# Second network weight's butterflies on GpSimd in the second attention, third raw weight buffer for the experts

## The chip, the cores and the metric

The kernel runs on one core of a Trainium2 chip. The engines are TensorE (PE), VectorE (DVE), ScalarE (ACT), GpSimd (POOL) and SyncE (SP), with 16 DMA engines. DMAs are issued by SP, by ACT (small ones) and by POOL (the indirect ones). The metric is the device time of one execution in microseconds; lower is better.

## The reference, cut to what matters

A decoder of two layers on `x` of shape (4, 512, 512) in float32. Each layer has three steps, each on the layernorm of what came before and added to it:

```python
x = x + _L0_attn_ref(_layernorm(x), ...)             # attention with a linear memory, 16 heads
x = x + _L0_xattn_ref(ctx_512, _layernorm(x), ...)   # learned graph over the tokens
x = x + _L0_ffn_ref(_layernorm(x), ...)              # experts: 32 routed, top 8 of 64, 512 -> 2*256 -> 512
x = x + _L1_attn_ref(_layernorm(x), ...)             # attention
x = x + _L1_xattn_ref(_layernorm(x), ctx_512, ...)   # causal attention over the context
x = x + _L1_ffn_ref(_layernorm(x), ...)              # network 512 -> 2048 -> 512 with a Hadamard transform
```

The last one is `hidden = silu(x @ W1.T) * (x @ W3.T)`, then `out = fwht(hidden) @ W2.T`. `fwht` is the Walsh-Hadamard transform over the 2048 hidden columns: in 11 rounds it takes pairs `a`, `b` to `a + b` and `a - b`. It is linear, so the kernel applies it to the weight W2 in place of `hidden`. An expert computes `silu(g) * u` from `x @ w_gate_up`, and multiplies by `w_down`.

## The kernel before, in words

Six stages follow each other, each with its own block of code per engine: `attention_linear` (0 to about 680 us), `graph_and_router` (to about 1103 us), `experts` (to about 1488 us), `attention_layers` (two attentions, self and causal, to about 2425 us) and `network`. Engines are ordered by semaphores alone; each engine runs its instructions in the order written. SP issues one DMA after the other, and whatever it waits for holds up everything behind it; POOL likewise, where compute and indirect DMAs are one queue.

**The second network weight.** W2 (512 by 2048) is transformed in two parts. In the graph stage "asides" do the first 7 rounds: TensorE multiplies transposed chunks of 128 hidden columns by a 128x128 Hadamard matrix, ACT scales the result into one of three buffers `aside_out` (128 x 512), and SP stores it to `w2T` in HBM (`aside_store`, 16 stores of 256 KB). The last 4 rounds (`STAGES`) mix the 16 chunks. Before, this was done in `experts`: SP loads a tile of 128 output columns of all 16 chunks (`load_w2`, 1 MB in 512-byte pieces, 4 tiles) into `shared_rows`, DVE does 4 stages of two instructions each (`butterfly`, one instruction after each of the 32 experts, 128 x 1024 elements) between the two halves of `shared_x`, and SP stores the result to `w2_mixed` (`store_w2`, 1 MB), which the network reads.

**The experts.** For each of 32 experts e, in the order of TensorE: transposes of the gathered rows of e+2 (L2367), gate and up products of e+1 (48 matmuls in three passes of high and low parts, L50 to L52), down products of e (12). Weights come raw from HBM by SP (`first_gu`, 1 MB, and `first_d`, 512 KB, two buffers each, by the parity of e), ACT casts the high part (L2419, L2423), DVE subtracts for the low part of gate-up (L2455), POOL for the low part of down (L2518). Gate-up's and down's loads of an expert both wait (L2327, L2328, in Signal's L176) until DVE and POOL have split the expert two before. POOL's order for expert e is

```python
gather(e + 4)                      # two indirect DMAs, rows of x into ex_rows
split_d(e // 2 + 1, e % 2)         # the low part of down's weights, expert e + 2
scatter(e)                         # waits for y of e and for the landing of scatter e - 1
```

where the scatter adds 256 rows of y to `x_rows` in HBM. ACT and DVE write the gated y (L2441, L2486) into SBUF, two buffers.

**The attentions.** 32 steps g (8 batches, of which 4 are causal, times 4 groups of 4 heads), with lead-in steps from -3. In step g TensorE does the scores of g (L440) for the exponentials of ACT, the scores of g+1 (L420) for the maxima of DVE (L657), the weighed values and sums of g (L454, L463), at the end of the step the maxima's transpose (L431) and the projections of g+3. Three pairs of PSUM banks go round. ACT copies the weighed values and sums of g-1 at the start of step g (L604, L607); before the copy of values it waits until POOL has made `oT` of g-2 in the step before. DVE takes reciprocals of the sums (L682) and POOL multiplies them into `oT` (L766), once a step. The output projection of a batch (L532) follows in the first step of the next batch (steps 5, 9, ...), after POOL's `oT` of its last group. POOL also makes `rstd` once a batch, and masks in the causal half. SP's `stack` issues 12 DMAs of 128 KB (L336) for the scores of g+3 at the end of each step.

## Time and profile before

| | us |
|---|---|
| median of 3 timed runs | 2962.68 (2962.14 to 2963.93) |
| the profiled execution | 2967.87 |
| its span, first to last instruction | 2966.1 |

| engine | busy us | share of the span |
|---|---|---|
| TensorE matmul | 2490.3 | 84% |
| DVE | 1781.1 | 60% |
| ACT | 1225.8 | 41% |
| POOL | 791.4 | 27% |

Mean granted clock of TensorE 0.908 of full speed. The busy shares are means over stages with different limits, so they have to be read stage by stage. The durations of single instructions in the text are those of the profiled execution, which took 5.2 us more than the median.

### The profile page before, as it was taken

The numbers are of one execution on the slowest core, as the hardware profiler recorded it, in microseconds if no ns is written. First come the engines' busy times: TensorE is split into PE (matmuls) and PEld (weight loads), VectorE is DVE, ScalarE is ACT, GpSimd is POOL, SyncE is SP. The second block draws the span as 40 slices with busy tenths as digits, with TensorE's granted clock in tenths as the row PEclk, the third lists the DMA queues.
The fourth block names the chain that finished last, engine by engine and source line by source line (L and its number), as shares of the span: only waits on it lengthen the run. The fifth ranks groups of instructions, "written<-read, shape, count | busy, mean of one in ns | idle before, by whom it ended". The sixth has DMA issues, their size and how long they took to land. (4 is left out here: it accounts for less than half of the span.)

```text
span 2966.1 us, 34593 instructions
## 1 busy us (share of the span) xinstructions
PE 2490.3 (84%) x12822; PEld 1652.2 (56%) x12822; DVE 1781.1 (60%) x2772; ACT 1225.8 (41%) x1859; POOL 791.4 (27%) x1054
## 2 busy tenths in 40 slices
PE   5899999984344369889769999999999879999999
PEld 4554545421222248788645454545555548888887
DVE  3766666546799977777636655655565444444443
ACT  3343434335766725455314333443433223333332
POOL 2223232213566626878600000001211110000000
PEclk8999999986666679999879999999999889999999
DMA  3313132202222357999732323333533331101000
GB/s 108 77 44 86 44 86 47 68 19 94 85 94 90 111 186 221 268 255 268 188 95 65 93 72 78 91 97 94 128 88 94 115 125 67 43 1 43 1 29 15
DMA packets 177017, 287.09 MB, mean 97 GB/s; under 512 B 20769, under 2 KB 52385, under 8 KB 176866
## 3 DMA queue, kind: packets, MB, share of 16 engines
q1 hardware_dynamic: 159458, 249.73, 28.7%
q0 software_dynamic: 14336, 34.61, 5.4%
q8 instruction: 88, 1.44, 0.2%
q10 hardware_dynamic: 3072, 0.79, 0.1%
q14 instruction: 63, 0.52, 0.1%
HBM read 149.79 MB, written 58.98 MB: 70 GB/s over the span
## 5 line engine op out<-in xcount | busy, mean ns | idle before, releaser
L657 DVE TENSOR_REDUCE at_negmax<-at_ps 128x2 f32<-128x1024 f32 (+3 forms) x256 | 259.2, 1017 | 131.5 <-PE at_ps L420 66.6
L572 ACT ACTIVATE at_probs<-at_ps 128x1024 f32<-128x1024 f32 (+3 forms) x256 | 221.8, 866 | 265.3 <-PE at_ps L440 262.5
L1258 DVE TENSOR_REDUCE a_negmax<-a_ps 128x2 f32<-128x1024 f32 x128 | 155.2, 1217 | 137.4 <-PE a_ps L1011 136.8
L50 PE MATMUL ff_ps<-ff_xnT_hi,ff_s_hi 128*128 128x512 f32 x512 | 201.0, 393 | 5.1 <-DVE ff_xnT_lo L2782 5.1
L52 PE MATMUL ff_ps<-ff_xnT_hi,ff_s_lo 128*128 128x512 f32 x512 | 200.2, 391 | 0.0
L51 PE MATMUL ff_ps<-ff_xnT_lo,ff_s_hi 128*128 128x512 f32 x512 | 200.1, 391 | 0.0
L1842 ACT ACTIVATE gr_act_signs<-gr_signed,gr_test 128x512 bf16<-128x512 f32 x248 | 177.3, 717 | 25.6 <-POOL gr_test L2221 14.0
L1159 ACT ACTIVATE a_probs<-a_ps 128x1024 f32<-128x1024 f32 x128 | 130.9, 1024 | 137.8 <-PE a_ps L1029 137.3
L2812 DVE TENSOR_TENSOR ff_hid<-ff_hid,ff_ps 128x512 f32<-128x512 f32 x64 | 44.0, 688 | 238.8 <-ACT ff_hid L2757 238.8
L440 PE MATMUL at_ps<-at_qk 98*128 98x512 f32 (+3 forms) x512 | 171.7, 417 | 17.6 <-DMA at_qk<-at_mrow 10.8
L440 PEld LDWEIGHTS at_ps<-at_qk 98*128 98x128 f32 x512 | 83.1, 193 | 158.7 <-issue 89.9
L420 PE MATMUL at_ps<-at_qk 96*128 96x512 f32 (+3 forms) x512 | 161.0, 378 | 11.7 <-DVE at_xnT_lo L718 8.0
L2757 ACT ACTIVATE ff_hid<-ff_ps 128x512 f32<-128x512 f32 x64 | 38.3, 598 | 303.6 <-PE ff_ps L52 303.6
L50 PE MATMUL ex_ps<-ex_x_hi,ex_gu_hi 128*128 128x256 f32 x512 | 151.5, 296 | 4.9 <-issue 4.9
L2536 POOL DMA_INDIRECT x_rows<-ex_y,ex_index_out x64 | 134.7, 2104 | 56.0 <-DMA x_rows<-ex_y,ex_index_out 38.8
L51 PE MATMUL ex_ps<-ex_x_lo,ex_gu_hi 128*128 128x256 f32 x512 | 148.3, 290 | 0.0
L52 PE MATMUL ex_ps<-ex_x_hi,ex_gu_lo 128*128 128x256 f32 x512 | 147.9, 289 | 0.0
L766 POOL TENSOR_TENSOR at_oT<-at_weighed 128x512 f32<-128x512 f32 x32 | 40.8, 1274 | 382.4 <-DVE at_weighed L682 382.4
L750 POOL TENSOR_SCALAR_AFFINE_SELECT at_probs<-at_probs 128x256 f32<-128x256 f32 x128 | 52.6, 412 | 291.6 <-ACT at_probs L572 291.6
L682 DVE RECIPROCAL at_weighed<-at_weighed 128x128 f32<-128x128 f32 x128 | 119.9, 940 | 15.3 <-ACT at_weighed L607 15.3
L727 DVE TENSOR_TENSOR at_part<-at_ps,at_part 128x512 fp32r<-128x512 f32 x64 | 43.4, 692 | 142.3 <-ACT at_part L628 142.3
L532 PE MATMUL at_ps<-at_wo,at_oT 128*128 128x512 f32 x256 | 115.9, 607 | 6.8 <-POOL at_oT L766 6.6
(416 smaller groups left out, 6425.9 us busy)
## 6 DMA issues: line engine op xcount, KB each, us to landing
at_qk<-at_part SPq DMA_DIRECT2D x384, 128.0 KB, 2.3
first_gu<-in_L_ffn_w_gate_up_dram SPq DMA_DIRECT2D x32, 1024.0 KB, 6.2
a_qk<-a_part SPq DMA_DIRECT2D x192, 128.0 KB, 2.3
first_d<-in_L_ffn_w_down_dram SPq DMA_DIRECT2D x32, 512.0 KB, 7.8
gr_aside_raw<-in_L_ffn_W_dram SPq DMA_DIRECT2D x48, 256.0 KB, 3.3
w13T<-gr_aside_out SPq DMA_DIRECT2D x32, 256.0 KB, 3.2
shared_x<-x_after_cross SPq DMA_DIRECT2D x8, 1024.0 KB, 8.0
ff_slab<-w13T SPq DMA_DIRECT2D x14, 512.0 KB, 6.3
```

Of the source, the lines that this page charges most:

```text
L50: pe.matmul(out, lh, rh, start=start, stop=False, skip_group_check=True)
L51: pe.matmul(out, lh, rl, start=False, stop=False, skip_group_check=True)
L52: return pe.matmul(out, ll, rh, start=False, stop=stop, skip_group_check=True)
L420: mm = pe.matmul(bank(key, i, 0, n), qk[0:KROWS, g % STACKS, 0, j, t * P:(t + 1) * P], qk[0:KROWS, g % STACKS, 1, j, 0:n], start=True, sto ...
L440: mm = pe.matmul(bank(key, i, lo), qk[0:KROWS + 2, g % STACKS, 1, j, t * P:(t + 1) * P], qk[0:KROWS + 2, g % STACKS, 0, j, lo:S], start=Tr ...
L572: act.activation(probs[:, t % 2, 2 * w:2 * w + 2, lo:S], banks(("kq", g, s), lo), ACT.Exp, scale=SCALE).then_inc(free(("kq", g, s)), 1)
L657: dve.reduce_max(negmax[:, g % 2, :].rearrange("p (j t) -> p j t", t=NT)[:, 2 * w:2 * w + 2, t], banks(("qk", g, s), 0, width(g, t)), AX.X ...
L682: dve.reciprocal(weighed[:, 1, t * P:(t + 1) * P], weighed[:, 1, t * P:(t + 1) * P]).then_inc(rec_done, 1)
L1159: act.activation(probs[:, t % 2, 2 * w:2 * w + 2, :], banks(("kq", g, s)), ACT.Exp, scale=SCALE).then_inc(free(("kq", g, s)), 1)
L1258: dve.reduce_max(negmax[:, g % 2, :].rearrange("p (j t) -> p j t", t=NT)[:, 2 * w:2 * w + 2, t], banks(("qk", g, s)), AX.X, negate=True).t ...
L1842: act.activation(act_signs[:, j, :], src, ACT.Sign, scale=-1.0, bias=against, accum_out=total[:, i, j:j + 1]).then_inc(counted_to[j], 1)
L2536: pool.indirect_dma_start(x_rows, bass.IndirectOffsetOnAxis(index_out[:, at:at + 1], 0), y[:, u, t, :], None, compute_op=ALU.add).then_inc ...
```

## The change

Three things. First, the last 4 stages of the second weight leave the experts and go to POOL in the self attention, as 8 tiles of 64 output columns (`W2_COLS`), at steps -1, 0, 2, 3, 4, 6, 7 and 8. At each it runs 8 instructions of 128 x 512 elements, before `oT` of that step. SP loads the next tile (512 KB, now whole rows of 4 KB, as `w2T` has a new layout) and stores the finished one (512 KB in 256-byte pieces) at the head of a step. The second stage of a tile waits for the previous tile's store, since its buffer is overwritten. Second, the asides' stores to `w2T` go in 256-byte pieces, to fit the new layout. Third, the experts' raw weights get a third buffer in `shared_x`, and the buffers are taken by e modulo 3; the gate-up load waits for DVE's split of expert e-3 alone, the down load for POOL's. The network's loads of its first chunks also wait for the last store.

```diff
+        W2_STEPS = (-1, 0, 2, 3, 4, 6, 7, 8)
+        w2_raw, mix = got[:, 0].rearrange("p k d -> p (k d)"), [got[:, 1 + i].rearrange("p k d -> p (k d)") for i in range(2)]
...
+            def load_w2(n):
+                if n:
+                    sp.wait_ge(mixed, 2 * STAGES * (n - 1) + 2)
+                sp.dma_start(w2_raw, w2T.rearrange("(t p) e -> t p e", p=P)[n]).then_inc(w2_in, 16)
+
+            def store_w2(n):
+                sp.wait_ge(mixed, 2 * STAGES * (n + 1))
+                sp.dma_start(w2_mixed.rearrange("(k p) (t c) -> t p k c", p=P, c=W2_COLS)[n],
+                             mix[(STAGES - 1) % 2].rearrange("p (k c) -> p k c", c=W2_COLS)).then_inc(w2_out, 16)
...
+                sp.wait_ge(w2_out, 16 * len(W2_STEPS))
...
             load(sp, 0)
             load(sp, 1)
+            load_w2(0)
             for g in STEPS:
                 b, c = g // NC, g % NC
+                if g - 1 in W2_STEPS:
+                    store_w2(W2_STEPS.index(g - 1))
+                if g in W2_STEPS[:-1]:
+                    load_w2(W2_STEPS.index(g) + 1)
...
+            def butterflies(n):
+                for stage in range(STAGES):
+                    src, dst = mix[(stage - 1) % 2] if stage else w2_raw, mix[stage % 2]
+                    a, b, c, d = (m.rearrange("p (g h k) -> p g h k", h=2, k=W2_COLS << stage)[:, :, h, :] for m in (src, dst) for h in range(2))
+                    if stage == 0:
+                        pool.wait_ge(w2_in, 16 * (n + 1))
+                    if stage == 1 and n:
+                        pool.wait_ge(w2_out, 16 * n)
+                    if n or stage:
+                        pool.wait_ge(mixed, 2 * (STAGES * n + stage))
+                    pool.tensor_tensor(c, a, b, ALU.add).then_inc(mixed, 1)
+                    pool.tensor_tensor(d, a, b, ALU.subtract).then_inc(mixed, 1)
+
             rstds(0)
             for g in STEPS:
+                if g in W2_STEPS:
+                    butterflies(W2_STEPS.index(g))
...
-            w13_parts, w2_parts = w13T.rearrange("(k p) (m e) -> k m p e", p=P, m=2), w2T.rearrange("(k p) d -> k p d", p=P)
+            w13_parts, w2_parts = w13T.rearrange("(k p) (m e) -> k m p e", p=P, m=2), w2T.rearrange("(t p) (k c) -> k p t c", p=P, c=W2_COLS)
...
+        raw_gu, raw_d = [first_gu[:, 0], first_gu[:, 1], shared_x[:, 0]], [first_d[:, 0], first_d[:, 1], shared_x[:, 1, 0:I_DIM // P, :]]
+        RAWS = len(raw_gu)
...
-            load(1, 0)
-            load_w2(0)
-            for i in range(PAIRS - 2):
-                load(i + 1, 1)
-                load(i + 2, 0)
-                if i % STAGES == 2:
-                    load_w2(i // STAGES + 1)
-                if i % STAGES == 0 and i:
-                    store_w2(i // STAGES - 1)
-            load(PAIRS - 1, 1)
-            store_w2(NT - 1)
-            sp.wait_ge(w2_out, 16 * NT)
+            def load(e):
+                r, i, u = e % RAWS, (e - RAWS) // 2, (e - RAWS) % 2
+                if e >= RAWS:
+                    gu_lo_done[u].wait(sp, i, 1)
+                sp.dma_start(raw_gu[r], gu_dram[e]).then_inc(w_in[r], 16)
+                if e >= RAWS:
+                    d_lo_done[u].wait(sp, i, 1)
+                sp.dma_start(raw_d[r], d_dram[e]).then_inc(w_in[r], 16)
...
             for e in range(E_ROUTED):
                 body(e // 2, e % 2, e + 2 < E_ROUTED)
-                butterfly(e)
```

## Rows read from the trace of the kernel before

**Rows 1.** Windows: from:to, length, busy (x instructions) by engine, clock, DMA share, GB/s.
```profile
1106.00:1150.00 44.00, 33.36 (x213) 31.59 (x214) 23.12 (x20) 19.93 (x20) 24.07 (x15) 0.77 0.61 193
1150.00:1440.00 290.00, 263.55 (x1815) 242.82 (x1814) 224.92 (x186) 149.71 (x160) 233.38 (x133) 0.95 0.96 263
1440.00:1489.00 49.00, 26.93 (x153) 22.49 (x151) 25.05 (x20) 10.81 (x14) 23.86 (x13) 0.81 0.58 112
...
1640.00:1760.00 120.00, 116.87 (x574) 61.16 (x573) 67.16 (x84) 44.79 (x52) 6.12 (x5) 1.00 0.30 77
```

**Rows 2.** Groups of lines, 1150 to 1440: busy us, mean ns | idle before, ended by.
```profile
L2536 POOL DMA_INDIRECT x_rows<-ex_y,ex_index_out x52 | 111.2, 2139 | 39.8 <-DMA x_rows<-ex_y,ex_index_out 29.7 <-issue 10.1
...
L2518 POOL TENSOR_TENSOR ex_d_lo<-first_d,ex_d_hi 128x1024 fp32r<-128x1024 f32 x27 | 65.2, 2415 | 0.6
L2545 POOL DMA_INDIRECT ex_rows<-normed,index x54 | 58.1, 1075 | 16.5 <-issue 16.5
L2419 ACT CAST ex_gu_hi<-first_gu 128x2048 fp32r<-128x2048 f32 x27 | 51.6, 1910 | 35.0 <-DMA first_d<-in_L_ffn_w_down_dram 35.0
...
L2367 PE MATMUL ex_ps<-ident,ex_rows 128*128 128x128 f32 x208 | 31.1, 298 | 23.1 <-DMA ex_rows<-normed,index 22.9 <-issue 0.2
...
L2498 DVE TENSOR_TENSOR shared_x<-shared_x 128x1024 f32<-128x1024 f32 x20 | 24.3, 1215 | 8.2 <-DMA w_mixed<-shared_x 8.2
...
L2498 DVE TENSOR_TENSOR shared_x<-shared_rows 128x1024 f32<-128x1024 f32 x7 | 8.5, 1211 | 0.0
```

**Rows 3.** Waits of SP, 1110 to 1480: us in total, times, longest.
```profile
SPq L176 <- POOL ex_d_lo L2518: 295.6, 30, 22.7
```

**Rows 4.** Timeline, one load: start, us, engine, line [idle before <-releaser].
```profile
1261.39 2.42 POOL L2518 TENSOR_TENSOR ex_d_lo<-first_d,ex_d_hi 128x1024 fp32r<-128x1024 f32 x1
...
1263.89 0.37 SPq L2329 DMA_DIRECT2D first_gu<-in_L_ffn_w_gate_up_dram  x1
...
1274.26 1.91 ACT L2419 CAST ex_gu_hi<-first_gu 128x2048 fp32r<-128x2048 f32 x1 [2.52 <-DMA first_d<-in_L_ffn_w_down_dram]
```

**Rows 5.** DMA, 1150 to 1440: packets; queues; issues with KB and landing us.
```profile
DMA packets 45266, 76.30 MB, mean 263 GB/s; under 512 B 2651, under 2 KB 14939, under 8 KB 45259
...
q1 hardware_dynamic: 33255, 47.31, 50.8%
q0 software_dynamic: 12004, 28.93, 45.1%
...
shared_rows<-w2T SPq DMA_DIRECT2D x3, 1024.0 KB, 15.0
...
x_rows<-ex_y,ex_index_out POOLq DMA_INDIRECT x52, 7.8
```

**Rows 6.** End of the experts: timeline of DVE, and waits of 1440 to 1490.
```profile
1444.49 4.37 DVE L2498 TENSOR_TENSOR shared_x<-shared_x 128x1024 f32<-128x1024 f32 x1
...
1455.75 4.38 DVE L2498 TENSOR_TENSOR shared_x<-shared_x 128x1024 f32<-128x1024 f32 x1
...
PE ex_ps L50 <- DVE ex_h_lo L2455: 5.9, 3, 3.9
```

**Rows 7.** Attention: POOL by line; timelines of POOL, SP, ACT; landings.
```profile
L766 POOL TENSOR_TENSOR at_oT<-at_weighed 128x512 f32<-128x512 f32 x32 | 40.8, 1274 | 382.4 <-DVE at_weighed L682 382.4
...
1677.14 1.28 POOL L766 TENSOR_TENSOR at_oT<-at_weighed 128x512 f32<-128x512 f32 x1 [23.06 <-DVE at_weighed L682]
...
1663.52 7.63 SPq L336 DMA_DIRECT2D at_qk<-at_part  x12
...
1687.87 0.59 ACT L604 COPY at_weighed<-at_ps 128x512 f32<-128x512 f32 x1 [0.46 <-PE at_ps L454]
...
w2T<-gr_aside_out SPq DMA_DIRECT2D x16, 256.0 KB, 2.0
...
x_after_attn<-at_res SPq DMA_DIRECT2D x8, 512.0 KB, 2.9
```

More of the change, by code:

```diff
@@ L21 @@
 HID = 2048
+W2_COLS = 64
 HC = P // HD
@@ L241, in attention_layers @@
         staged, ctx_sb = got[:, 0], got[:, 1, 0, :].rearrange("p (t l) -> p t l", l=L)
+        STAGES = (HID // P).bit_length() - 1
+        W2_STEPS = (-1, 0, 2, 3, 4, 6, 7, 8)
+        assert len(W2_STEPS) == D // W2_COLS and W2_STEPS[-1] < NC * (B - 2) + 1
+        w2_raw, mix = got[:, 0].rearrange("p k d -> p (k d)"), [got[:, 1 + i].rearrange("p k d -> p (k d)") for i in range(2)]
+        w2_in, w2_out, mixed = sem("w2_in"), sem("w2_out"), sem("mixed")
         above, above_r = got[:, 1, 1, 0:P], wkT[0][:, 1, 0:P]
@@ L2274, with experts @@
 I_DIM = 256
-def experts(nc, env, tag, normed, index, x_rows, w_gate_up, w_down, w2T, w2_mixed, raw_gu, raw_d, shared_x, shared_rows):
+def experts(nc, env, tag, normed, index, x_rows, w_gate_up, w_down, first_gu, first_d, shared_x, shared_rows):
     F = 2 * I_DIM // P
@@ L2322, in _ @@
         def _(sp):
-            def load(i, u, weights=True):
-                e = i * 2 + u
-                if not weights:
-                    return
-                gu_lo_done[u].wait(sp, i, 0)
-                d_lo_done[u].wait(sp, i, 0)
-                sp.dma_start(raw_gu[:, u], gu_dram[bass.ds(e, 1)].rearrange("e p c f -> (e p) c f")).then_inc(w_in[u].sem, 16)
-                sp.dma_start(raw_d[:, u], d_dram[bass.ds(e, 1)].rearrange("e p c f -> (e p) c f")).then_inc(w_in[u].sem, 16)
-            def load_w2(n):
-                if n:
-                    sp.wait_ge(mixed, 2 * STAGES * (n - 1) + 2)
-                sp.dma_start(w2_raw[:].rearrange("p (k c) -> p k c", c=P), w2_tiles[n]).then_inc(w2_in, 16)
-            def store_w2(n):
-                sp.wait_ge(mixed, 2 * STAGES * (n + 1))
-                sp.dma_start(mixed_tiles[n], mix[:, (STAGES - 1) % 2, :].rearrange("p (k c) -> p k c", c=P)).then_inc(w2_out, 16)
-            for u in range(2):
-                load(0, u, weights=False)
-                sp.sem_inc(w_in[u].sem, 32)
-            load(1, 0)
-            load_w2(0)
-            for i in range(PAIRS - 2):
-                load(i + 1, 1)
-                load(i + 2, 0)
-                if i % STAGES == 2:
-                    load_w2(i // STAGES + 1)
-                if i % STAGES == 0 and i:
-                    store_w2(i // STAGES - 1)
-            load(PAIRS - 1, 1)
-            store_w2(NT - 1)
-            sp.wait_ge(w2_out, 16 * NT)
+            def load(e):
[6 more added lines that the diff above has]
+                sp.dma_start(raw_d[r], d_dram[e]).then_inc(w_in[r], 16)
+            for r in range(2):
+                sp.sem_inc(w_in[r], 32)
+            for e in range(2, E_ROUTED):
+                load(e)
         @block.tensor
@@ L2416, in split_gu @@
             def split_gu(i, u):
-                w_in[u].wait(act, i, 32)
+                e = 2 * i + u
+                act.wait_ge(w_in[e % RAWS], 32 * (e // RAWS + 1))
                 gu_ready[u].wait(act, i, 0)
-                act.copy(flat(gu_hi[:, u]), flat(raw_gu[:, u])).then_inc(gu_hi_done[u].sem, 1)
+                act.copy(flat(gu_hi[:, u]), flat(raw_gu[(2 * i + u) % RAWS])).then_inc(gu_hi_done[u].sem, 1)
             def split_down(i, u):
                 y_ready[u].wait(act, i, 0)
-                act.copy(flat(d_hi[:, u]), flat(raw_d[:, u])).then_inc(d_hi_done[u].sem, 1)
+                act.copy(flat(d_hi[:, u]), flat(raw_d[(2 * i + u) % RAWS])).then_inc(d_hi_done[u].sem, 1)
             def split_x(i, u):
@@ L2458, in split_gu @@
                 gu_hi_done[u].wait(dve, i, 1)
-                low(flat(gu_lo[:, u]), flat(raw_gu[:, u]), flat(gu_hi[:, u]), gu_lo_done[u])
+                low(flat(gu_lo[:, u]), flat(raw_gu[(2 * i + u) % RAWS]), flat(gu_hi[:, u]), gu_lo_done[u])
             def keep_gate(i, u):
@@ L2486, in body @@
                 dve.tensor_scalar(y[:, u, 1, :], ps[:, 7, :], gate[:, (2 * i + u) % 4, 1:2], None, ALU.mult).then_inc(y_dve[u].sem, 1)
-            def butterfly(n):
-                row, stage, half = n // (2 * STAGES), n // 2 % STAGES, n % 2
-                src, dst = mix[:, (stage - 1) % 2, :] if stage else w2_raw[:], mix[:, stage % 2, :]
-                a, b, c, d = (m.rearrange("p (g h k) -> p g h k", h=2, k=P << stage)[:, :, h, :] for m in (src, dst) for h in range(2))
-                if stage == 0 and half == 0:
-                    dve.wait_ge(w2_in, 16 * (row + 1))
-                if stage == 1 and half == 0 and row:
-                    dve.wait_ge(w2_out, 16 * row)
-                if n:
-                    dve.wait_ge(mixed, n)
-                dve.tensor_tensor((c, d)[half], a, b, (ALU.add, ALU.subtract)[half]).then_inc(mixed, 1)
             dve.tensor_scalar(empty[:], index[:], 0.5, None, ALU.is_lt).then_inc(emptied, 1)
@@ L2517, in split_d @@
                 d_hi_done[u].wait(pool, i, 1)
-                pool.tensor_tensor(flat(d_lo[:, u]), flat(raw_d[:, u]), flat(d_hi[:, u]).bitcast(F32), ALU.subtract
+                pool.tensor_tensor(flat(d_lo[:, u]), flat(raw_d[(2 * i + u) % RAWS]), flat(d_hi[:, u]).bitcast(F32), ALU.subtract
                                    ).then_inc(d_lo_done[u].sem, 1)
```

22 lines of the change are left out of this document (11 added, 11 removed).

## The prediction

> **What bounds the kernel now.** I read the busy table by stage first, because the change touches three stages and leaves the rest alone. In the experts' steady part, 1150 to 1440 us, four things stand close together [rows 1]: TensorE is busy 263.6 of 290 us at a granted clock of 0.95 (of the 2.4 GHz level), the DMA engines 0.96 of the time at 263 GB/s, POOL 233.4 us, DVE 224.9 us. In the attention that follows (1640 to 1760) it is TensorE alone, 116.9 of 120 us at clock 1.00, with POOL at 6.1 us.
>
> Next I read the groups of lines of that steady part, for what ended each idle time [rows 2]. TensorE's waits of any size there are 22.9 us of the transposes L2367, for gathered rows that have not landed. Those gathers are issued by POOL, and POOL is nearly full: its 233.4 us of work and 27 us of issue gaps (10.1 + 16.5 + 0.6, the idle in front of L2536, L2545 and L2518; L2536's is 39.8 less 29.7 of DMA) make 260.6, and the other 29.7 us it waits for the previous expert's scatter to land. ACT meanwhile waits 35.0 us at L2419 for raw weights. About 26.6 experts pass here (L2419 27 times, L2536 52 times two to an expert), so an expert takes 10.9 us.
>
> Why the weights are late stands in the waits of SP [rows 3] and in one stretch of time [rows 4]. SP waits 295.6 us, 30 times, always for POOL's `d_lo` split, since both loads of an expert wait for it. POOL does that split at 1261.39 to 1263.81, SP issues the load at 1263.89, and ACT's cast of the next expert but one, which uses that buffer, stands at 1274.26 after 2.52 us of waiting. So in practice a load has one period to land, not two.
>
> The DMA section of the same stretch says how full the engines are and with what [rows 5]: queue q1 takes 50.8% of 16 engines, q0 (gathers and scatters) 45.1%. The second weight's tiles go in pieces of 512 bytes: 3 loads and 3 stores of 1 MB, that is 12,288 packets and 6.29 MB of q1's 33,255 and 47.31. One such load lands after 15.0 us.
>
> **The change, part by part, and what it costs.**
>
> *Experts, steady part.* Removed: 27 DVE butterflies at 1.21 us, 32.8 us, and the 8.2 us that they waited for the store [rows 2]; six of the eight 1 MB transfers. DVE is not the bound, so the 41 us are no gain as such. What counts is the DMA demand. By bytes the w2 pieces are 6.29/47.31 of 50.8%, or 6.8% of the engines' 290 us, 19.6 us. By packets it would be 12,288/33,255, 54 us; a 512-byte piece surely takes less time than a 2 KB one, so I take the bytes. If the DMA engines stay at 0.96, 19.6 us less demand shortens the part by 20.4 us. Moved: the three-deep ring lets expert e's load start after the split of e-3, and its gate-up half no longer waits for POOL's split. That gives a load one period (10.9 us) more; the longest wait in [rows 4] was 2.5 us, so I expect the 35.0 us of ACT to go entirely. What is late next is POOL: 260.6 us of work and gaps, then TensorE at 263.6. So 26.4 us is the ceiling and 0 the floor, if scatter's landing keeps its pace. I take 17: the 20.4, less a sixth, since three resources within 3% of each other do not all run full. Term: -17.
>
> *Experts, both ends.* At the start SP loads w2 (1 MB) in front of expert 3's weights; at 263 GB/s that is 4 us of engine time. Part of it is hidden, I take -2 (bounds 0 and -4). At the end two butterflies last 4.4 us in place of 1.2 [rows 6], because POOL's split of two SBUF tensors runs at the same time; `hid` of the next expert stands behind them, and TensorE waits 5.9 us in three places for `h_lo`. With the butterflies gone I take -4 (bounds 0 and -8: the 5.9 and some 2 us of the last 1 MB store, which runs beside the last scatters). Term: -6.
>
> The Trainium skill (SBUF — State Buffer, Who interferes with whom) says that a DVE instruction with two SBUF inputs and a GpSimd instruction that reads SBUF shut each other out. The 4.4 against 1.2 us of [rows 6] agrees. By it the move takes two-input work off DVE where POOL is full, and in attention the DVE lines that could meet the butterflies are few, since maxima, splits and residuals read PSUM; it leaves the sum as it is.
>
> *Attention, POOL.* Added: 8 tiles of 8 instructions over 128x512. POOL's product of two SBUF tensors of that shape, L766, takes 1.27 us [rows 7], so 64 x 1.274 = 82 us, 10.2 a tile, on an engine that is idle 113.9 of 120 us. Queued behind them on POOL: `oT` of the step before and `rstd`. Who waits: ACT's copy L604 and the output projection. The narrow places are tiles 4 and 7 (steps 4 and 8). In step 4 the store of tile 3 is issued by SP only after the twelve `stack` DMAs, at 1671.2; butterflies after the first stage wait for it. If it lands 5 us after, six more instructions end at 1683.8, and `oT`, now at 1677.1, ends at 1685.1. ACT's copy stands at 1687.9 [rows 7]. That is 2.8 us of slack. Landing of a store of this size from attention is 2.9 us with 2 KB pieces, and 15.0 is the worst that any w2 transfer shows [rows 5, 7]. At 15 us `oT` would end at 1695.1: 7.2 us late, twice; with 1.3 us each for tiles 3 and 6, an estimate (their step leaves more room), 17 us together. I take 5 us to land and no loss there, and 1 us for SP's 16 more issues and 8 MB more traffic. Term: +1 (bounds 0 and +17).
>
> The Trainium skill (DMA: Bandwidth & Descriptors, Specifications) wants pieces of 512 bytes or more, with read-modify-write below; here w2 goes to HBM in 256-byte pieces in two places. This speaks against the change; no row of this trace has a 256-byte store. Were such a store twice as slow as the 2.9 us one, 5.8 us, it would still end inside the slack.
>
> *Attention, the rest.* The reciprocals and the layernorm of DVE read SBUF alone, one tensor each, and may meet butterflies. `rstd` stands behind tiles 1, 4 and 7 on POOL and is used only in the next step. SP's new wait in front of the network's chunks is for stores that end at step 9 of 34. I take 0, and keep as the far end that each butterfly delays DVE by its whole length, 82 us.
>
> *Graph stage.* Sixteen stores of 256 KB of the second weight now go in 256-byte pieces. They land in 2.0 us now [rows 7]; three output buffers cover them, and even 4 us is shorter than the spacing of three asides. I take 0, bounds 0 and 16 x 1 us.
>
> **Sum.** -17 - 6 + 1 + 0 = -22 us. The profiled execution took 2967.9 us (span 2966.1), so 2945.9; it lies 5.2 us above the median of the three timed runs, 2962.7, which gives 2940.7.
>
> **Rivals.**
>
> *The scatter chain holds the pace.* Each scatter waits for the previous one's landing; one issue of 2.1 us, then the second's landing of 7.8 us make 9.9 us [rows 2, 5], near the period of 10.9 already. Then ACT's wait for weights goes and POOL's stays. For it: the 29.7 us [rows 2]. Against: landing depends on the same full DMA engines. It leaves 5 of the 17: -10, 2952.7. Chance 0.17.
>
> *TensorE's floor is reached.* All 26.4 us of idle go, ends -8, attention 0: -34, 2928. For it: no resource but POOL is then above TensorE. Against: POOL's 260.6. Chance 0.13.
>
> *oT is late in attention.* The 256-byte store lands in 15 us: +17 in place of +1, so -6, 2956.7, no change that can be measured. It decides from 7.8 us of landing on. Against: the DMA engines are little used there. Chance 0.07.
>
> *DVE is held by POOL in attention.* This one ends slower. If POOL's butterflies shut DVE out for their whole length, 82 us of DVE are added over eight steps. TensorE waits for DVE's maxima bank by bank, with 3 banks to cover; with half of it exposed, +41 on -22 is +19, 2982. It decides once more than 22 us are exposed. For it: [rows 6]. Against: there both instructions read two SBUF tensors, and DVE's large lines in attention read PSUM. Chance 0.06.
>
> **How the numbers follow.** My forecast has 0.57; its own range is -10 to -32, 2931 to 2953. Range for 8 in 10: from 2928 (the TensorE floor) to 2957, which takes in the scatter chain and late `oT`. A measurement of this kernel tells 0.2%, 5.9 us, from no change. Faster than 2956.8: the forecast, the floor, and nearly all of the scatter case, 0.85; within 0.2%: most of late `oT` and the rest of the scatter case, 0.08; slower 0.07.
>
> **What the profile after would show.** Right: the experts' stage shorter by some 23 us; no wait of L2419 for first_d; DMA share still above 0.93 with fewer bytes; TensorE's share there above 0.95; in attention 64 POOL instructions near 1.27 us and TensorE's steps unchanged. Wrong: L2536 still waiting 30 us for its own landing, L604 or L532 waiting for `oT`, or DVE's maxima L657 and reciprocals L682 longer than before. The prediction fails most easily at the 17, which rests on how three nearly full resources share what is freed.

## The result, and the profile after

The changed kernel takes 2970.41 us (median), the kernel before 2960.11 us in the runs beside it: ratio 1.0031, 95% interval 1.0021 to 1.0040. It is slower by 0.3%, where 0.7% faster was forecast, and outside the forecast range. The profiled execution has a span of 2977.0 us against 2966.1.

One number first on how far single profiles carry. In eighteen later profiles the code ahead of the experts is the same, and yet the experts' first instruction stands anywhere from 1094.8 to 1109.6 us. So I compare lengths of stages, and let medians of many runs decide on the whole. A stage's length varies too: a second profile of the same changed kernel (`after_again`) has 381.2 us for the experts where the first has 389.6, so a difference of a few us between two single profiles is no result by itself.

The borders of the stages are single instructions: the experts' iota, the next block's first load, the first `stack` (here of the kernel after; before they stand at 1103.51, 1488.65 and 1515.73):

```profile
1104.08 0.14 POOL L2553 IOTA ex_spare_rows<- 128x2 int32 x1 [43.27 <-POOLq L45]
```

```profile
1493.65 0.92 SPq L225 DMA_DIRECT2D shared_x<-x_rows  x2
...
1523.56 6.42 SPq L342 DMA_DIRECT2D at_qk<-at_part  x10
```

The experts' stage takes 1493.65 - 1104.08 = 389.6 us (before 385.1; 381.2 in `after_again`), where some 23 less were forecast. From there to the first `stack` of the attention it is 29.9 us (before 27.1). The rest, up to the feed-forward's cast of `xnT_hi`, is 914.3 us (before 911.2; kernels with the same code there lie between 909.9 and 914.3, so these 3.1 us are no result).

The busy table of the steady part, to be read beside [rows 1]: length, busy us (x instructions) of PE, PEld, DVE, ACT and POOL, granted clock, DMA share, GB/s.

```profile
1150.00:1440.00 290.00, 256.66 (x1780) 234.49 (x1778) 211.42 (x157) 144.09 (x157) 205.28 (x130) 0.97 0.93 238
```

The groups of lines of the same stretch, which answer to [rows 2]:

```profile
L2542 POOL DMA_INDIRECT x_rows<-ex_y,ex_index_out x52 | 90.0, 1730 | 68.5 <-DMA x_rows<-ex_y,ex_index_out 60.6 <-issue 7.9
...
L2474 DVE TENSOR_TENSOR ex_gu_lo<-first_gu,ex_gu_hi 128x2048 fp32r<-128x2048 f32 x18 | 79.7, 4430 | 9.7 <-ACT ex_gu_hi L2438 9.7
...
L2385 PE MATMUL ex_ps<-ident,ex_rows 128*128 128x128 f32 x208 | 30.1, 291 | 33.3 <-DMA ex_rows<-normed,index 33.3
```

And its transfers, which answer to [rows 5]:

```profile
DMA packets 32365, 68.92 MB, mean 238 GB/s; under 512 B 2483, under 2 KB 2483, under 8 KB 32358
...
q1 hardware_dynamic: 20717, 40.75, 48.1%
q0 software_dynamic: 11641, 28.11, 45.1%
...
first_gu<-in_L_ffn_w_gate_up_dram SPq DMA_DIRECT2D x18, 1024.0 KB, 7.8
first_d<-in_L_ffn_w_down_dram SPq DMA_DIRECT2D x18, 512.0 KB, 4.4
...
x_rows<-ex_y,ex_index_out POOLq DMA_INDIRECT x52, 8.2
ex_rows<-normed,index POOLq DMA_INDIRECT x52, 6.2
```

What the reader is to see: the work did go away (DVE 13.5 us less, 7.4 MB less, no line waits for weights), and yet no more experts pass: 52 scatters, as before. From the end of one expert's second scatter issue to the next's it is 11.17 us on average (before 11.04, a little more than the prediction's 10.9; 10.93 in `after_again`), worked out from POOL's timelines. I call this the spacing. DMA share fell only from 0.96 to 0.93 while the rate fell from 263 to 238 GB/s. POOL now waits 60.6 us for its own scatters (29.7 before), TensorE 33.3 us for gathered rows (22.9), and `gu_lo` takes 4.43 us where it took 2.81 (the line of the kernel before):

```profile
L2455 DVE TENSOR_TENSOR ex_gu_lo<-first_gu,ex_gu_hi 128x2048 fp32r<-128x2048 f32 x26 | 73.1, 2810 | 30.5 <-ACT ex_gu_hi L2419 30.5
```

A gate-up load lands in 7.8 us (6.2 before), a scatter in 8.2 (7.8), gathered rows in 6.2 (5.5).

At the attention's start, the timeline of the kernel after:

```profile
1503.62 1.25 POOL L785 TENSOR_TENSOR shared_rows<-shared_rows 128x512 f32<-128x512 f32 x1
1503.67 5.70 DVE L671 TENSOR_SCALAR shared_x<-shared_x,at_mv,at_rstd 128x512 f32<-128x512 f32 x4 [1.17 <-POOL at_rstd L766]
1504.84 1.44 POOL L786 TENSOR_TENSOR shared_rows<-shared_rows 128x512 f32<-128x512 f32 x1
```

The four layernorm instructions of DVE take 5.70 us together, in the kernel before 1.92:

```profile
1498.55 1.92 DVE L649 TENSOR_SCALAR shared_x<-shared_x,at_mv,at_rstd 128x512 f32<-128x512 f32 x4 [1.17 <-POOL at_rstd L744]
```

GpSimd's first butterfly starts 0.05 us ahead of them.

### The profile page after: what moved, and what is told of

The parts are those of the page before. It is cut to its first block and busy times, and to the rows that moved or that the text cites. A ratio compares the mean times of both kernels' runs of the same rounds, so it can differ in the third digit from the quotient of the medians.

```text
span 2977.0 us, 34609 instructions
## 1 busy us (share of the span) xinstructions
PE 2487.8 (84%) x12822; PEld 1647.6 (55%) x12822; DVE 1765.1 (59%) x2740; ACT 1223.5 (41%) x1859; POOL 846.0 (28%) x1118
## 5 line engine op out<-in xcount | busy, mean ns | idle before, releaser
L1884 ACT ACTIVATE gr_act_signs<-gr_signed,gr_test 128x512 bf16<-128x512 f32 x248 | 177.3, 717 | 25.4 <-POOL gr_test L2263 10.6
L2542 POOL DMA_INDIRECT x_rows<-ex_y,ex_index_out x64 | 112.9, 1764 | 82.9 <-DMA x_rows<-ex_y,ex_index_out 72.8
L476 PE MATMUL at_ps<-at_probs,at_v 128*32 128x512 f32 (+3 forms) x1024 | 118.9, 537 | 0.7 <-POOL at_probs L772 0.5
```

The costliest lines, as they stand in the source:

```text
L476: mm = pe.matmul(ps[j * HD:(j + 1) * HD, NUM, lo:S], v[:, g // NC % 2, t, c * P + j * HD:c * P + (j + 1) * HD], probs[:, t % 2, j, lo:S], ...
L1884: act.activation(act_signs[:, j, :], src, ACT.Sign, scale=-1.0, bias=against, accum_out=total[:, i, j:j + 1]).then_inc(counted_to[j], 1)
```

## Experiments

"Stage" is from the experts' iota to the next block's first load, in one profile; "landing" the median of scatters and of gathers in 1150 to 1440; "GU" how long after the end of the last gather's issue SyncE issues the gate-up load, in most periods (worked out from the timelines of POOL and SP); the ratio is to the kernel before, with its 95% interval.

| version | ratio | stage us | landing us | GU us |
|---|---|---|---|---|
| before | 1 | 385.1 | 7.8, 5.5 | 2.5 |
| after | 1.0031 (1.0021-1.0040) | 389.6 | 8.2, 6.2 | 4.6 |
| after_again | 1.0020 (1.0007-1.0033) | 381.2 | 8.0, 6.0 | 4.6 |
| two_raw | 0.9975 (0.9962-0.9987) | 373.4 | 7.1, 5.1 | 2.5 |
| paired | 0.9983 (0.9971-0.9995) | 375.2 | 7.5, 5.5 | 2.5 |
| start_wait | 1.0024 (1.0011-1.0037) | 382.7 | 8.1, 6.2 | 4.6 |
| norm_first | 1.0007 (0.9994-1.0020) | 381.3 | 8.1, 6.2 | 4.6 |
| split_two | 1.0008 (0.9998-1.0017) | 381.3 | 8.2, 6.1 | 4.6 |
| late_down | 0.9985 (0.9974-0.9995) | 376.7 | 7.5, 5.4 | 2.5; nine at 2.8-5.1 |
| d_first | 0.9997 (0.9987-1.0007) | 374.3 | 7.7, 5.5 | 2.9 |
| gu_delayed | 1.0003 (0.9993-1.0013) | 376.0 | 7.9, 5.6 | 3.0 |
| both_late | 0.9990 (0.9979-1.0000) | 375.2 | 7.6, 5.5 | 2.5 |
| gu_landing | 0.9992 (0.9978-1.0006) | 374.6 | 7.7, 5.6 | 2.9 |
| both_landing | 0.9979 (0.9967-0.9991) | 373.6 | 7.9, 5.7 | 2.5-4.5 |
| apart | 1.0026 (1.0012-1.0041) | 388.6 | 8.5, 6.3 | 4.9 |
| pair_then_split | 1.0015 (1.0000-1.0029) | 380.6 | | |
| split_then_pair | 1.0010 (0.9995-1.0025) | 377.3 | | |
| no_weights | 2947.1 us, one run | 363.2 | 5.2, 4.8 | |
| two_norm | 0.9970 (0.9960-0.9980) | 371.4 | 7.2, 4.9 | 2.5 |
| three_norm | 0.9970 (0.9958-0.9982) | 373.5 | 7.5, 5.4 | 2.5 |

The versions fall into two groups. "Split" are those in which the gate-up load waits for `gu_lo` alone throughout: after, after_again, start_wait, norm_first, split_two, apart. "Paired" are the ten, other than no_weights, in which both loads wait for both low parts. In 1150 to 1440 the spacing is 10.93 to 11.17 us in the six split profiles and 10.59 to 10.69 in the ten paired ones, and POOL waits 46.9 to 62.5 us for its scatters to land in the split ones, 12.3 to 25.2 in the paired ones (29.7 before). These two measures part the groups more clearly than the length of the stage.

### The change taken apart: two_raw and paired

The pairing, in both:

```diff
                 if e >= RAWS:
                     gu_lo_done[u].wait(sp, i, 1)
+                    d_lo_done[u].wait(sp, i, 1)
                 sp.dma_start(raw_gu[r], gu_dram[e]).then_inc(w_in[r], 16)
-                if e >= RAWS:
-                    d_lo_done[u].wait(sp, i, 1)
                 sp.dma_start(raw_d[r], d_dram[e]).then_inc(w_in[r], 16)
```

and in two_raw `raw_gu, raw_d = [first_gu[:, 0], first_gu[:, 1]], [first_d[:, 0], first_d[:, 1]]`.

> The changed kernel with two raw weight buffers and the old pairing (both low parts read, then both loads issued); what is left of the change is that the second network weight's transfers and butterflies are in the attention. Theory crowding (mine now): the third buffer buys nothing, because the pace of the steady part is that of the row traffic and the scatters, and its earlier loads lengthen gathers and scatters. Then the first transposes come back from 1114.2 to about 1110, the experts' stage falls from 389.6 us to 376 to 384, and the kernel is 5 to 13 us faster than the changed one (about 2957 to 2965). Rival, buffer is worth it: the weights wait of ScalarE (35 us before) comes back, the stage grows to 393 us or more, and the kernel is slower than the changed one.

> Three raw buffers, but from the fourth load on both loads of an expert wait for both low parts, as before; the third buffer's first load stays early. Theory alignment: the gate-up load that now goes 6 to 8 us ahead of the down load crowds the scatters and gathers and brings gu_lo on VectorE (4.43 us mean now, 2.81 before) into GpSimd's d_lo; with the pair together gu_lo falls to about 3 us, the stage shrinks by 3 to 8 us. Rival, scatter chain alone: the stage stays within 2 us of 389.6, since the chain of scatter issue and landing doesn't depend on when the weights go. The start stays late (1114) by both.

Both are faster than the kernel before, and 13 to 16 us (medians) faster than the changed one. Both moved the way their theories said, and further: the stages of 373.4 and 375.2 us are shorter than either expectation had them, and `gu_lo` came down to 3.1 and 3.5 us on average. The waits of two_raw in 1150 to 1440 (total us, times, longest) hold the surprise:

```profile
ACT ex_gu_hi L2437 <- DMA first_d<-in_L_ffn_w_down_dram: 64.3, 26, 5.6
...
PE ex_ps L2384 <- DMA ex_rows<-normed,index: 24.3, 22, 1.8
...
POOL x_rows L2541 <- DMA x_rows<-ex_y,ex_index_out: 15.2, 11, 2.4
```

ScalarE's wait for weights is 64.3 us, nearly twice the 35.0 of [rows 2], and yet the stage is the shortest so far, at 55 scatters (27.5 experts) in 290 us. In the paired version that wait does not appear and the stage is no shorter. So the wait that the third buffer was to remove lay beside the path. The w2 work moved out is worth 385.14 - 373.36 = 11.8 us, one profile each; the medians agree (0.25% faster in all, 7.4 us, with some 3 us lost at the attention's start). The third buffer by itself is worth nothing that shows: 333.2 us against 333.8 from the first scatter on, and 2.4 us lost ahead of it. What remains between paired and the changed kernel, 6 us (after_again) to 14 us (after), is the price of letting each load go behind its own reader.

### The experts' start: start_wait

```diff
+            turned[0].wait(sp, 0, 1)
             for e in range(2, E_ROUTED):
                 load(e)
```

> The changed kernel, but SyncE issues the first weight load only when the first expert's rows are turned. Theory: the load at 1106.1 beside the first gathers makes them land 4.3 us late, so the first transposes return to 1110 and the whole stage ends 3 to 5 us earlier; kernel 3 to 5 us faster than the changed one. Rival: the late start is taken up by the pace of the steady part anyway (or the load then comes too late for the third expert), the stage's end moves by under 1 us.

In the kernel after the third buffer is free at once, and its load meets the first gathers; these are rows of the timelines of SP, POOL and ACT:

```profile
1106.08 0.37 SPq L2365 DMA_DIRECT2D shared_x<-in_L_ffn_w_gate_up_dram  x1
```

```profile
1104.98 1.27 POOL L2551 DMA_INDIRECT ex_rows<-normed,index  x1 [0.77 <-SPq L172]
1106.55 0.95 POOL L2551 DMA_INDIRECT ex_rows<-normed,index  x1 [0.30 <-issue]
```

```profile
1116.18 1.01 ACT L2446 CAST ex_x_hi<-ex_ps 128x1024 fp32r<-128x1024 f32 x1 [7.36 <-PE ex_ps L2385]
```

With the wait, ACT's `ex_x_hi` stands 8.3 us behind the iota (1109.78 - 1101.45) instead of 12.1, and the first scatter 39.5 instead of 42.9 us (41.3 in `after_again`):

```profile
1109.78 1.01 ACT L2447 CAST ex_x_hi<-ex_ps 128x1024 fp32r<-128x1024 f32 x1 [3.58 <-PE ex_ps L2386]
```

So the expectation holds in its place. Its size, 3 to 5 us of the whole kernel, is not shown: the median is 5 us below the first measurement of the changed kernel, but `after_again`, the same kernel without the wait, has the ratio 1.0020 against the 1.0024 here.

### The attention's start: norm_first

```diff
             rstds(0)
+            pool.wait_ge(xn_done, NT)
             for g in STEPS:
                 if g in W2_STEPS:
                     butterflies(W2_STEPS.index(g))
```

> The changed kernel, but GpSimd's first butterflies wait until VectorE has normalised the first batch. Theory: GpSimd held VectorE's four layernorm instructions at 5.70 us instead of 1.92, on the path; they return to about 1.9 us and the first stack comes 3.8 us after the block's start earlier; kernel 3.5 to 6 us faster than the changed one. Rival: the layernorm was late for its statistics or rows, not for GpSimd, or the butterflies, now later, hold the first store and stack by as much: within 1 us of the changed kernel.

The timeline of norm_first at the attention's start:

```profile
1485.92 1.92 DVE L671 TENSOR_SCALAR shared_x<-shared_x,at_mv,at_rstd 128x512 f32<-128x512 f32 x4 [1.17 <-POOL at_rstd L766]
...
1487.91 1.27 POOL L785 TENSOR_TENSOR shared_rows<-shared_rows 128x512 f32<-128x512 f32 x1 [2.03 <-DVE shared_x L671]
```

The layernorm is back at 1.92 us, the butterflies stand behind it, and from the block's first load to the first `stack` it is 25.7 us instead of 29.9. The median is 8 us below the first measurement of the changed kernel; only 4.2 of it can be placed here. Against `after_again` the ratio is 0.13% lower, 4 us, which fits.

### Does the split order cost with two buffers too: split_two, late_down

split_two has two raw buffers and the changed kernel's waits. late_down has three buffers, the pair's waits, and in front of the down load

```diff
+                if e >= 5:
+                    y_out[(e - 5) % 2].wait(sp, (e - 5) // 2, 16 * CT)
```

> Two raw buffers, but each load waits for its own reader alone, as in the changed kernel: the gate-up load goes some 6 us ahead of the down load. Beside the kernel with two raw buffers and the old pairing (experts' stage 373.4 us, from the first scatter to the next block's first load 333.8), this differs in the pairing alone. Theory, the split order costs: the stretch after the first scatter grows by 6 to 14 us, to 340 to 348, in spite of weights that are in earlier, with longer packets of both queues. Rival, the split hurts only together with the third buffer (then a load is always ready to go): with two buffers it stays within 3 us of 333.8 or falls, since the wait for weights (64 us) gets shorter.

> Three raw buffers; the gate-up load waits for both low parts, as in the paired version, but the down load waits further until a scatter has landed, some 5 to 7 us later. Weights are in time all the same. Theory, two bursts instead of one: the loads are mixed with row traffic in more places, packets get longer, and the stretch after the first scatter is 339 us or more where the paired version had 333.2. Rival, the cost of the changed kernel is a gate-up load that goes too early, and not the splitting: then this stays within 3 us of 333.2.

split_two stands 0.33% above two_raw, with a spacing of 11.02 us against 10.68: the third buffer is not needed for the loss. The stage is 7.9 us longer. From the first scatter on it is 345.9 against 333.8 us, but 4.2 of these 12.1 are a first scatter that came earlier. late_down fell to its rival: with the down load late and the gate-up load with the pair's timing, 333.0 us. Two bursts instead of one cost nothing.

### When and in which order the loads go: d_first, gu_delayed, both_late

d_first swaps the two `dma_start` of the pair; gu_delayed does that and puts these waits between them; both_late has them ahead of both loads, gate-up first:

```diff
+                if e >= 5:
+                    y_act[(e - 5) % 2].wait(sp, (e - 5) // 2, 1)
+                    y_dve[(e - 5) % 2].wait(sp, (e - 5) // 2, 1)
```

> Three raw buffers, both loads of an expert together once both low parts are read, but the down load ahead of the gate-up load. Lengths are from the first scatter to the next block's first load: 346.7 us in the changed kernel, 333.2 in the paired version with the gate-up load ahead. Theory, lateness: what costs in the changed kernel is that the gate-up load gets going some 2 us after the down load and runs into the scatter; here it is behind it by only 0.4 us of issue, so the length stays within 3 us of 333.2. Rival, order: with 0.5 MB of the down load ahead of it, the 1 MB of the gate-up load moves among the scatter's packets in either case, and the length is 341 or more.

> As the version with the down load ahead, but the gate-up load waits further until the scatter is about to be issued (both halves of the scaled result written). Theory, lateness: 340 us or more from the first scatter on, gate-up landings near 7.8 us and scatter landings near 8.2, as in the changed kernel. Rival, the changed kernel's loss comes from GpSimd holding VectorE's gu_lo (5.1 us in place of 2.3) or from which reader each load waits for, not from when the traffic goes: within 3 us of 333.2.

> Three raw buffers, gate-up load first, but both loads wait until the scatter is about to be issued. Theory, lateness: the whole 1.5 MB then shares the engines with the scatter, so this is the slowest or as slow as the changed kernel, 342 us or more from the first scatter on. Rival, it is only the spread of the loads over the period that costs: one burst, wherever it starts, stays within 4 us of 333.2.

From the first scatter on they take 330.9, 332.7 and 332.2 us, as the pair does, with the pair's spacing (10.59 to 10.62). So d_first came out as expected, and gu_delayed and both_late fell to their rivals. The column GU says why two of them are weaker tests than meant: the operands were ready ahead of `d_lo`, and the load went 2.5 to 3.0 us behind the gathers' issue, not the 4.6 of the changed kernel. The ratios of d_first and gu_delayed lie 0.14% and 0.20% above the pair's, at the edge of what the intervals part. So a small cost of the order, up to 0.2%, is not excluded by the medians, though the profiles show none.

### What the transfers are worth: no_weights

In two_raw both loads are replaced by `sp.sem_inc(w_in[r], 32)`; all experts then compute with the first two experts' weights.

> Two raw buffers, and all weight loads of the experts' loop after the first two experts are left out (each expert computes with the weights of the first two). Theory, transfers set the pace: the period of the last experts of every version, after the last load, is 7.2 to 8.4 us; here it is that from the start, and the experts' stage falls from 373 to 250 to 285 us. Rival, the chain of a scatter's issue and landing or an engine sets the pace by itself: the period stays above 9.5 us, the stage above 320.

Of no_weights, 1150 to 1440: the busy table, POOL's wait for its scatters, and the landings.

```profile
1150.00:1440.00 290.00, 269.20 (x1904) 246.16 (x1902) 187.91 (x168) 155.12 (x168) 256.71 (x137) 0.99 0.59 101
```

```profile
POOL x_rows L2540 <- DMA x_rows<-ex_y,ex_index_out: 3.7, 2, 2.0
```

```profile
x_rows<-ex_y,ex_index_out POOLq DMA_INDIRECT x57, 5.2
ex_rows<-normed,index POOLq DMA_INDIRECT x52, 4.8
```

My expectation failed by far, and the rival held (a stage above 320 us). With 42 MB less, a DMA share of 0.59 and scatters that land in 5.2 us, the stage is 363.2 us, only 10 below two_raw: 57 scatters, 28.5 experts, pass in 290 us where 27.5 did. TensorE is at 269.2 of 290 us and POOL at 256.7. So in this one profile it is the engines' own chain, not the weights, that sets the pace; which engine's is not shown. The 7 to 8 us at the end of every version are experts behind which no rows are gathered and no later expert's data is split. I had taken them for a pace that the middle could reach; it does not, at 10.24 us without any weight traffic.

### Step with the landing, and the hold: gu_landing, both_landing, apart, after_again

gu_landing loads down first and puts the wait between the loads, both_landing ahead of both, gate-up first:

```diff
+                if e >= 6:
+                    y_out[(e - 6) % 2].wait(sp, (e - 6) // 2, 16 * CT)
```

apart, in DVE's `split_gu` of the changed kernel:

```diff
+                if i:
+                    d_lo_done[(u + 1) % 2].wait(dve, i - 1 + u, 1)
```

> Three raw buffers, down load once both low parts are read, gate-up load only when the scatter before the next one has landed, which is what also releases the next scatter. Theory, locked in step: in the changed kernel each scatter waits for the landing of the one before, and the gate-up load always goes beside it, so the 1 MB shares the engines with every scatter, its landing gets longer and the backlog never clears. Then this has the changed kernel's pace: experts' stage 381 us or more, scatter landings near 8.2 us, GpSimd's wait for landings 50 us or more in 290. Rival: the stage stays at 374 to 377, and the step between loads and scatters is not the cause.

> As before, but both loads wait for that landing. Theory, locked in step: as slow or slower, 381 us or more. Rival, only a burst that is split in two costs (down load before, gate-up load after): 374 to 377.

> The changed kernel, but VectorE begins gu_lo only when GpSimd has finished the d_lo that it met. Theory, the hold costs nothing by itself (gu_lo then ends at the same time): gu_lo falls from 4.4 to about 2.3 us, the stage and the time stay within 3 us of the changed kernel. Rival, the hold is the cause of the split order's loss: the stage falls to 375 and the time by 8 us or more.

> The changed kernel once more. Expected: ratio to the kernel before between 1.001 and 1.005; the experts' stage anywhere in 381 to 390 us. If it is below 378, the stage's cost of the split order rests on chance, and only the medians of many runs count.

Both landing versions fell to their rival, 374.6 and 373.6 us. For gu_landing this says little: its gate-up load went 2.9 to 3.0 us behind the gathers' issue, as in d_first, in 23 of 26 periods, so the landing was there already and its wait held nothing back. In both_landing the wait did hold: the loads went 2.5 to 4.5 us behind, and scatters and gathers landed in 7.9 and 5.7 us, near the 8.0 and 6.0 of `after_again`, and the stage is one of the shortest all the same. In apart `gu_lo` is 2.3 us in every period and the stage is 388.6 us: the length of the held instruction costs nothing by itself, as expected. But the load behind it still goes 4.9 us after the gathers' issue, for `gu_lo` ends where it ended before.

### Each expert, or a state: pair_then_split, split_then_pair

The extra wait of the pair under `e < 17` in the one and `e >= 17` in the other, and the separate wait under the opposite condition.

> Three raw buffers, loads in pairs up to expert 16, each behind its own reader from expert 17 on (its loads go at about 1270 us). Theory, a cost at each expert: scatters come 10.3 to 10.5 us apart before the change of order and 10.9 to 11.3 us apart behind it; GpSimd's wait for landings goes from under 1 us to over 2 us each. Rival, a state entered at the start: the second half keeps 10.3 to 10.5 us, since the pipeline never got into it.

> The other way round. Cost at each expert: 10.9 to 11.3 us apart first, 10.3 to 10.5 us behind the change. State entered at the start: 10.9 us or more in both halves.

POOL's group of scatters before and behind the change of order (1150 to 1270, 1290 to 1440; busy, mean ns, idle and what ended it), first pair_then_split:

```profile
L2544 POOL DMA_INDIRECT x_rows<-ex_y,ex_index_out x22 | 43.7, 1985 | 10.4 <-issue 5.3 <-DMA x_rows<-ex_y,ex_index_out 5.2
```

```profile
L2544 POOL DMA_INDIRECT x_rows<-ex_y,ex_index_out x28 | 50.8, 1814 | 27.7 <-DMA x_rows<-ex_y,ex_index_out 23.1 <-issue 4.6
```

then split_then_pair:

```profile
L2544 POOL DMA_INDIRECT x_rows<-ex_y,ex_index_out x22 | 39.1, 1778 | 24.9 <-DMA x_rows<-ex_y,ex_index_out 20.8 <-issue 4.1
```

```profile
L2544 POOL DMA_INDIRECT x_rows<-ex_y,ex_index_out x28 | 53.8, 1923 | 16.3 <-DMA x_rows<-ex_y,ex_index_out 10.4 <-issue 5.9
```

The wait for a scatter's landing is 5.2 us for 11 experts with the pair and 23.1 for 14 behind the change to the split; the other way 20.8 for 11, then 10.4 for 14. The spacing in the same two stretches is 10.58, then 10.83 us in the one, 11.18, then 10.52 in the other; the expectations had 10.3 to 10.5 and 10.9 to 11.3. It comes and goes with the order. It is a cost at each expert, not a state entered at the start.

### Both repairs together: two_norm, three_norm

> Two raw buffers, paired loads, and the first butterflies only after the first layernorm. If the two gains are independent, 3.5 to 6 us below the version with two raw buffers and paired loads: ratio to the kernel before 0.9955 to 0.9965, about 2950 us. If the alone measured gain of the layernorm order (8 us between medians) was in part noise, 0.9965 to 0.9975.

> Three raw buffers, paired loads, the first weight load only once the first expert's rows are turned, and the first butterflies after the first layernorm. If the third buffer is worth nothing in the steady part, this stands within 2 us of the same with two raw buffers. If it was worth something that the late start hid (2.4 us to the first scatter), this is 2 us or more faster than that one.

Both stand at 0.9970: 0.30% faster than the kernel before and 0.5 to 0.6% faster than the changed one. The gain of the layernorm's order shows as 29.9 to 26.8 us in its place, but only as 0.05% between the ratios of two_raw and two_norm, the second case of the expectation. The third buffer adds nothing that shows, and two_norm is the version to keep.

## Why the prediction was wrong

**The step that failed** is the first term of the sum, -17 for the experts' steady part. From the first scatter on, the stage measured 346.7 us (339.9 in `after_again`) against 344.9 before, and the spacing 11.17 and 10.93 us against 11.04: nothing was gained. It failed in three places.

*"its gate-up half no longer waits for POOL's split"* was entered as part of the gain. It is the loss. Every split version has a stage of 381 to 390 us and a spacing of 10.9 to 11.2; every paired one 371 to 377 us and 10.6 to 10.7, with two buffers or three. I had looked at what the wait kept late (ACT's cast) and not at what it kept apart. Here are the queue's loads and the scatter behind them in the changed kernel, and in two_raw:

```profile
1299.72 5.13 DVE L2474 TENSOR_TENSOR ex_gu_lo<-shared_x,ex_gu_hi 128x2048 fp32r<-128x2048 f32 x1 [0.58 <-ACT ex_gu_hi L2438]
...
1300.29 2.40 POOL L2524 TENSOR_TENSOR ex_d_lo<-first_d,ex_d_hi 128x1024 fp32r<-128x1024 f32 x1
...
1302.71 0.37 SPq L2368 DMA_DIRECT2D first_d<-in_L_ffn_w_down_dram  x1
...
1304.87 0.37 SPq L2365 DMA_DIRECT2D shared_x<-in_L_ffn_w_gate_up_dram  x1
...
1305.95 1.62 POOL L2542 DMA_INDIRECT x_rows<-ex_y,ex_index_out  x1 [3.27 <-DMA x_rows<-ex_y,ex_index_out]
```

```profile
1298.10 2.41 POOL L2523 TENSOR_TENSOR ex_d_lo<-first_d,ex_d_hi 128x1024 fp32r<-128x1024 f32 x1
...
1300.58 0.37 SPq L2366 DMA_DIRECT2D first_gu<-in_L_ffn_w_gate_up_dram  x1
...
1300.99 0.63 SPq L2367 DMA_DIRECT2D first_d<-in_L_ffn_w_down_dram  x1
...
1301.61 2.54 POOL L2541 DMA_INDIRECT x_rows<-ex_y,ex_index_out  x1 [1.10 <-DMA x_rows<-ex_y,ex_index_out]
```

In the changed kernel `gu_lo` starts beside `d_lo` and takes 5.13 us, more than its own 2.3 (every period of apart) and POOL's 2.40 together; the 1 MB load behind it goes 2.2 us after the down load of the expert before and 4.6 us after the gathers' issue (it is the next expert's load, and its own down load follows 9.6 us later, at 1314.50), and the scatter waited 3.27 us for the one before. In two_raw both loads go at the end of `d_lo`, 2.5 us after the gathers' issue. That the late gate-up load is what costs is argued, not shown, and two rows speak against it as the whole cause: both_landing, with loads up to 4.5 us behind the gathers' issue and scatters that land in 7.9 us, and late_down, with nine gate-up loads at 2.8 to 5.1 us, keep the paired spacing (10.64 us in both). No version put a paired load that late throughout, and none let `gu_lo` end early throughout in the split order, so these two stay open as the cause. Shown is that the split order costs, at each expert, with either number of buffers. In the profiles the load order, the two bursts and the length of `gu_lo` cost nothing.

*"I expect the 35.0 us of ACT to go entirely ... So 26.4 us is the ceiling"*. The wait did go, and it was worth nothing: two_raw has 64.3 us of it. The ceiling was drawn from the idle time of single engines, as if each could be filled. no_weights gives a better one: with no weight transfer and no w2 work the stage is 385.1 - 363.2 = 22 us shorter, in one profile. My -23 for the stage asked for all that the transfers' total disappearance gave. Moving w2 out alone was worth 11.8 us, half of that.

*Demand by bytes.* I took DMA share as demand. Per packet q1 took 0.481 x 290 x 16 / 20,717 = 108 ns in the changed kernel, and in two_raw, with packets of the same sizes, 96 ns:

```profile
q1 hardware_dynamic: 21601, 42.47, 44.9%
```

Worked out the same way it is 105 to 108 ns in the six split profiles and 96 to 101 in the ten paired ones. So a byte has no fixed price in share, and fewer bytes need not mean a lower one: with a tenth fewer bytes than before it fell only from 0.96 to 0.93.

*The prediction's floor.* Its rival "TensorE's floor" said that no resource but POOL was above TensorE; its own numbers have POOL at 260.6 us, below TensorE's 263.6. Nothing of the outcome hangs on it.

**The ends (-6).** The start term had the wrong sign: -2 was taken, +2.6 measured to the first scatter (42.9 against 40.3; +1.0 in `after_again`), for the free buffer's load met the first gathers; start_wait takes it back. The tail's -4 was too large: from the end of the fourth-last expert's scatter issue to the next block's first load it is 32.1 us before, 31.0 after and 29.9 in `after_again`, so the butterflies' going gave 1 to 2 us there.

**Attention, POOL (+1).** The mechanism was right; a term of 1 us can't be told from the spread. The rows of tiles 3 and 4 and of the whole stretch:

```profile
w_mixed<-shared_rows SPq DMA_DIRECT2D x2, 512.0 KB, 4.5
```

```profile
1640.00:1760.00 120.00, 116.87 (x576) 60.57 (x575) 68.10 (x84) 45.44 (x52) 36.20 (x29) 1.00 0.41 106
```

```profile
L785 POOL TENSOR_TENSOR shared_rows<-shared_rows 128x512 f32<-128x512 f32 x12 | 15.4, 1282 | 37.1 <-DMA w_mixed<-shared_rows 36.5
```

The 256-byte store lands in 4.5 us where 5 were taken, a butterfly takes 1.28 us, and TensorE is busy 116.87 us, the same number as in [rows 1]. Late `oT` did not happen: behind the butterflies of tile 4 it ended at 1695.35, 3.2 us ahead of ACT's copy at 1698.56, where 2.8 us of slack were forecast.

**Attention, the rest (0).** Wrong by 2.8 us. The prediction let the layernorm meet butterflies because it reads only one tensor from SBUF. Its four instructions took 1.4 us each on average in place of 0.5, beside four butterflies. The Trainium skill (SBUF — State Buffer, Who interferes with whom) names `tensor_scalar` among the operations that can take the port pair shared with GpSimd, in a two-port mode; I had used only its rule on two inputs. The trace agrees: 5.70 us against 1.92. The reciprocals did not suffer (943 ns before, 942 after, in 1510 to 1900).

**The graph stage (0).** The stores to `w2T` land in 2.6 us instead of 2.0, as the median of the sixteen. The iota stands 0.6 us later, far inside the spread of that point; nothing shows.

**The rivals.** The scatter chain was the right mechanism, POOL waits 60.6 us for it in 26 experts, and it was priced as a remainder of the gain, where the change itself made the landings longer. "DVE is held by POOL in attention" named the right conflict and the wrong instructions: DVE's maxima read PSUM and kept 1.22 us; the layernorm was hit, once, for 3.8 us. TensorE's floor was not reached: even without weights TensorE is busy 269.2 of 290 us, at a stage of 363 us.

## What to carry to other kernels

A wait that looks too strict can be worth more than the time it costs, even where the reason can't be fully shown. Before it is loosened, note when the transfer will then go and what is on the DMA engines at that time; and when a change has such an edit and others in it, run it without that edit.

An upper bound of a gain is best measured by leaving the transfers out: one run without weights would have shown that a wait of 35 us on ScalarE and a full-looking DMA share were worth some 22 us together, to within the spread of one profile.

When work goes to GpSimd, list every DVE instruction that reads or writes SBUF where it lands, one-input ones too, and put it behind those that stand at the start of a stage, where nothing covers them.

## What the runs showed of the hardware

The same weight bytes in packets of the same size cost 105 to 108 ns a packet with split waits and 96 to 101 ns with paired ones, beside the same indirect row traffic.

GpSimd's 128x1024 subtraction (2.40 us) held VectorE's 128x2048 one for its whole length and some 0.4 us more: 2.3 us became 5.13. The other way round, the issue of an indirect scatter on GpSimd is 1.6 us alone and 3.5 us where it meets it (1402.46 in both_late); the scatters' issue is the largest item of POOL in every version (114.9 of 256.7 us with the weights left out).
